# A graph network's scatter of its sorted list, in three parts instead of two

## The chip, the core and the metric

One core of a Trainium2 chip runs the whole program. The metric is the device time of one execution in microseconds (us); lower is better. In a profile, PE is TensorE (PEld its weight loads), DVE VectorE, ACT ScalarE, POOL GpSimd, SP SyncE, and a trailing q marks an engine's sequencer.

## The reference

Four graph layers over 6250 nodes with 128 features and 106250 edges (`src`, `dst`, sorted by `dst`), each added to x after a layer norm and a relu:

```python
h = relu(layernorm(x)); x = x + L0(h)   # hyperbolic linear map, sum over edges, maps back
h = relu(layernorm(x)); x = x + L1(h)   # graph attention (4 heads, softmax per dst), then 25 spiking steps
h = relu(layernorm(x)); x = x + L2(h)   # per edge type: sums at dst of x[src], and at src of x[dst], dense
h = relu(layernorm(x)); x = x + L3(h)   # two weighted graph convolutions with layer norms
```

L1's spikes, for each node and feature, with the attention's output h:

```python
mem = 0.9 * mem + h; spk = mem > 1; mem = mem - spk      # 25 times; result sum(spk) / 25
```

L2 sums in both directions. The edges come sorted by `dst`, so the sum at `src` needs the same list sorted by `src`: the kernel sorts it itself.

## The kernel before

**Data.** Nodes lie in 49 blocks of 128 (NB = 49), in 7 groups of 7 blocks (NG, GB). The padded edges are 832 tiles of 128 (NT), four tiles to a chunk (CT), 208 chunks (NCH), and loops take four chunks a turn (RING), 52 turns (NIT).

**Walks.** Each walk gathers rows from a table in DRAM by 832 indirect DMAs, which GpSimd issues (`walk`, line 598), into a ring of four chunks in GATHERED. VectorE makes one-hot matrices (`onehots`, line 1278), TensorE multiplies them with the rows (`sums`, line 707, eight matmul records a chunk), and VectorE adds the PSUM bank to the block's sum (line 1300, in `aggregate`), then gives the buffer free (line 1322). Walks in order: l0, g1 (the scores' walk), l2, l2b, l3a, l3b. A walk waits until its table is stored.

**The sort.** Beside the l0 walk VectorE works out each edge's place in the list sorted by `src` (PLACE) and the pair to be stored there (REC: key and source). Then `scatter` (line 611) has GpSimd issue one indirect DMA a tile: 128 writes of 8 bytes from REC into `list_dram` at PLACE. Tiles go in batches of 16 (BATCH) on two semaphores in turn (`listed`), and before a batch GpSimd waits for the batch two before it. SyncE reads the list back into REC (line 553) once all are written; it is used from the l2b walk on.

**GpSimd's order around the change.** l0 walk; scatter of tiles 0 to 95 (EARLY = 96) beside the dense work of L1; g1 walk; scatter of tiles 96 to 831; wait for the typed table's stores (`typed_stored`); l2 walk; l2b walk; l3a and l3b.

**The stages beside it.** After the g1 walk (whose rows SyncE stored to `gat_rows` on the way), VectorE and TensorE work out the softmax maxima in unrolled code. The attention's pass ("gb") then goes over all chunks again in a loop: SyncE loads the chunk from `gat_rows` (line 543, 264 KB), ScalarE takes the exponentials (line 1012), VectorE weighs the rows (`weigh`, line 1654) and makes the one-hots, TensorE multiplies, VectorE adds (line 1300). Each addition raises `walks["gb"].added` by one, from 2 to NCH + 2. This pass needs nothing of GpSimd.

After it come the spikes, unrolled: 7 groups by 25 steps. In a step VectorE makes the new membrane and the reset in two halves (lines 1725 and 1729), ScalarE cuts off what is over the threshold (line 1046) and takes its sign (line 1017), and TensorE adds the spikes in PSUM with the identity (two matmuls, line 838). ScalarE's spike n waits with `spk_counted` for TensorE's spike n - 2. VectorE's membrane waits for ScalarE's line 1046 of the step before last. Beside the steps of group g, `typed_beside` does the dense work of L2 for group g - 1 (transposes at line 813, products at 820 and 828, copies at 1037), and SyncE stores each block's typed rows (line 549). The last of these 49 stores frees GpSimd for the l2 walk.

**The dense work of L1**, beside the early scatter: per group TensorE transposes (line 690), ScalarE copies (line 921), TensorE multiplies (line 697), ScalarE copies out (lines 934 and 935).

Of the kernel before, what the change touches and what calls it, by code (L numbers as in the profile page):

```python
# [58 lines left out]
def program(nc, x, src, dst, etype, weight, w0, b0, w1, att_src, att_dst, b1,  # L59
# [14 lines left out]
    NT = RP * RK  # L74
    NCH = NT // CT
# [19 lines left out]
    assert NB <= BUCKETS - 2  # L95
    BATCH = 16
    EARLY = 6 * BATCH
    assert NT % (2 * BATCH) == 0
    NBP = NB + 1
    NP3 = 3  # L100
# [15 lines left out]
    with ctx:  # L116
# [105 lines left out]
        class Walk:  # L222

            def __init__(self, n, gathers=True, adds=True, rounds=0, gathered=None, like=None):
# [4 lines left out]
                if not adds:  # L230
# [8 lines left out]
        walks = {"l0": Walk("l0"), "g1": Walk("g1", adds=False), "ga": Walk("ga", gathers=False, adds=False),  # L239
                 "gb": Walk("gb", gathers=False), "l2": Walk("l2")}  # L240
# [330 lines left out]
        @block.gpsimd  # L571
        def _(pool):
            pool.memset(ONE[:, :], 1.0).then_inc(s_const, 1)
            pool.memset(IDENT[:, :], 0.0).then_inc(s_const, 1)
            pool.memset(LOWER[:, :], 1.0).then_inc(s_const, 1)
            pool.iota(IOTA[:, :], pattern=[[1, NBP * P]], base=0, channel_multiplier=0,
                      allow_small_or_imprecise_dtypes=True).then_inc(s_const, 1)
            pool.iota(PB[:, :], pattern=[[P, NBP]], base=0, channel_multiplier=1,
                      allow_small_or_imprecise_dtypes=True).then_inc(s_const, 1)
            pool.wait_ge(s_const, 3)  # L580
            pool.affine_select(out=IDENT[:, :], in_=IDENT[:, :], compare_op=ALU.not_equal, fill=1.0,
                               base=0, pattern=[[-1, P]], channel_multiplier=1).then_inc(s_const, 1)

            pool.affine_select(out=LOWER[:, :], in_=LOWER[:, :], compare_op=ALU.is_gt, fill=0.0,
                               base=0, pattern=[[-1, P]], channel_multiplier=1).then_inc(s_const, 1)
            pool.iota(KCOL[:, :], pattern=[[1, BUCKETS]], base=0, channel_multiplier=0,
                      allow_small_or_imprecise_dtypes=True).then_inc(s_const, 1)
            pool.iota(CHUNK_AT[:, :], pattern=[[1, 1]], base=0, channel_multiplier=CE,
                      allow_small_or_imprecise_dtypes=True).then_inc(s_const, 1)

            def walk(name, table, width, rows):

                wk = walks[name]
                for c in range(NCH):
                    u = c % RING
                    pool.wait_ge(wk.free, c + 1)
                    for t in range(CT):
                        pool.indirect_dma_start(out=G3[:, u * CT + t, 0:width], out_offset=None, in_=table,  # L598
                                                in_offset=bass.IndirectOffsetOnAxis(
                                                    ap=rows[:, c * CT + t:c * CT + t + 1], axis=0),  # L600
                                                ).then_inc(wk.gathered[u], 16)

            pool.wait_ge(s_stored, 16)
            walk("l0", row_tabs[0], D, SRCI)
            def scatter(tiles):

                for t in tiles:
                    turn, k = divmod(t // BATCH, 2)
                    if t % BATCH == 0 and turn:
                        pool.wait_ge(listed[k], turn * (16 * BATCH))  # L610
                    pool.indirect_dma_start(out=list_dram,  # L611
                                            out_offset=bass.IndirectOffsetOnAxis(ap=PLACE[:, t:t + 1], axis=0),
                                            in_=REC[:, 2 * t:2 * t + 2], in_offset=None).then_inc(listed[k], 16)

            pool.wait_ge(placed, 1)
            scatter(range(EARLY))
            pool.wait_ge(s_stored, 16 * (NG + 1))
            walk("g1", gat_tab, XW, SRCI)
            scatter(range(EARLY, NT))

            for k in range(SLOTS):
                pool.wait_ge(typed_stored[k], 16 * len(range(k, NB, SLOTS)))
            walk("l2", typed_tab, D, KEYI)
            pool.wait_ge(nb_stored, 16 * (NB + 1))
            walk("l2b", typed_b_tab, D, PLACE)
            pool.wait_ge(s_stored, 16 * (2 * NG + 1))
            walk("l3a", row_tabs[1], D, SRCI)
            pool.wait_ge(s_stored, 16 * (3 * NG + 1))
            walk("l3b", row_tabs[2], D, SRCI)
# [1160 lines left out]
```

## Time and profile before

| what | us |
|---|---|
| device time, three runs | 10340.84, 10372.93, 10419.57 |
| median | 10372.93 |
| span of the profiled execution | 10508.5 |

The page gives no other time for the profiled execution than its span; nothing else of note lies around it, so the span is taken as its time. It is 1.3% over the median. "remote" as a releaser means that the profile found no event of this core that ended the wait; "issue" that it found nothing waited for.

### The profile page before, as it was taken

What the parts mean: (1) busy time and instruction counts of PE and PEld (TensorE: products, weight loads), DVE (VectorE), ACT (ScalarE), POOL (GpSimd) and SP (SyncE); (2) the same over time, 40 slices, a digit from 0 to 9 for tenths busy, and PEclk for the clock granted to TensorE, in tenths of its full rate; (3) what the DMA queues carried; (4) which work ended last, traced back from release to release, by engine and by line L of the source; (5) the groups of instructions that cost most, each with busy time, mean ns of one, the idle gap of its engine ahead of it and who ended that gap; (6) DMA issues with size and microseconds to landing.
All of it is one profiled execution on the core that took longest, in us unless ns stands there. A gap on an engine that the chain in (4) does not pass through costs nothing. (4 is left out here: it accounts for less than half of the span.)

```text
span 10508.5 us, 91849 instructions
## 1 busy us (share of the span) xinstructions
PE 3373.1 (32%) x14814; PEld 2819.9 (27%) x14815; DVE 3220.4 (31%) x6992; ACT 1117.8 (11%) x1899; POOL 5762.9 (55%) x5837
## 2 busy tenths in 40 slices
PE   1333431000010103654444443333333333333332
PEld 1333321000000003531233333333333233333332
DVE  5335553000020003579521221121222222422224
ACT  1000002222210000137300000000000000100000
POOL 0666775555567772000366666666655555455554
PEclk6555555555555555756666655555555555555555
DMA  1111112334320001310122221111111111111111
GB/s 39 48 44 42 44 34 74 105 103 106 102 66 11 10 11 49 85 42 28 50 57 56 55 55 42 45 43 45 41 48 40 41 40 41 40 40 40 41 41 40
DMA packets 335299, 521.81 MB, mean 50 GB/s; under 512 B 121171, under 2 KB 187559, under 8 KB 335199
## 3 DMA queue, kind: packets, MB, share of 16 engines
q0 software_dynamic: 186368, 330.08, 12.8%
q1 hardware_dynamic: 148831, 190.78, 5.9%
q14 instruction: 84, 0.69, 0.0%
q8 instruction: 16, 0.26, 0.0%
HBM read 421.31 MB, written 99.13 MB: 50 GB/s over the span
## 5 line engine op out<-in xcount | busy, mean ns | idle before, releaser
L707 PE MATMUL PS<-GATHERED,OH 128*128 128x128 f32 (+1 forms) x10240 | 2417.3, 417 | 4000.8 <-DVE OH L1278 1374.0
L598 POOL DMA_INDIRECT GATHERED<-row_tab,SRCI x2496 | 2465.6, 988 | 1866.8 <-issue 736.5
L707 PEld LDWEIGHTS PS<-GATHERED,OH 128*128 128x128 f32 x10240 | 2144.9, 312 | 4321.0 <-issue 1595.9
L598 POOL DMA_INDIRECT GATHERED<-typed_tab,KEYF x832 | 815.3, 980 | 1501.9 <-DMA typed_tab<-GATHERED 1096.3
L598 POOL DMA_INDIRECT GATHERED<-gat_tab,SRCI x832 | 788.0, 947 | 586.7 <-DVEq L1598 321.9
L598 POOL DMA_INDIRECT GATHERED<-typed_b_tab,PLACE x832 | 811.6, 975 | 430.1 <-issue 241.5
L611 POOL DMA_INDIRECT list_dram<-REC,PLACE x832 | 875.5, 1052 | 275.5 <-issue 275.5
L1284 DVE TENSOR_SCALAR OH<-IOTA,DSTF,WF 128x128 f32 x2048 | 609.4, 355 | 951.0 <-issue 917.8
L707 PE MATMUL PS<-T,OH 128*128 128x132 f32 x2048 | 446.8, 394 | 1065.3 <-issue 501.9
L707 PEld LDWEIGHTS PS<-T,OH 128*128 128x128 f32 x2048 | 400.2, 291 | 1111.9 <-issue 669.8
L1300 DVE TENSOR_TENSOR X<-X,PS 128x128 f32 x512 | 146.9, 287 | 1610.2 <-remote 993.6
L1300 DVE TENSOR_TENSOR ACC<-ACC,PS 128x129 f32 (+1 forms) x512 | 148.1, 289 | 1501.7 <-remote 1046.8
L1300 DVE TENSOR_TENSOR T<-T,PS 128x128 f32 x512 | 146.5, 286 | 1028.4 <-PE PS L707 457.9
L759 PE MATMUL PS<-AMP,EQ 128*128 x832 | 56.4, 177 | 1157.3 <-ACT EQ L978 871.6
L1278 DVE TENSOR_TENSOR OH<-IOTA,DSTF 128x512 f32 (+1 forms) x512 | 354.6, 693 | 146.1 <-issue 137.3
L759 PEld LDWEIGHTS PS<-AMP,EQ 128*128 128x128 bf16 x832 | 38.3, 107 | 1175.6 <-issue 1175.6
L1571 DVE TENSOR_REDUCE EX<-PS 128x48 f32 x208 | 43.2, 208 | 1006.0 <-issue 492.5
L900 ACT ACTIVATE H<-T,DINV 128x128 f32<-128x128 f32 x98 | 29.9, 394 | 2707.9 <-DVEq L56 2707.9
L974 ACT ACTIVATE SCR<-ROWI,SM 128x512 bf16<-128x512 int16 x208 | 150.0, 721 | 860.3 <-issue 850.3
L1278 DVE TENSOR_TENSOR OH<-IOTA,REC 128x512 f32 (+1 forms) x256 | 177.6, 694 | 197.2 <-issue 195.5
L838 PE MATMUL PS<-ACC,WSB 128*128 128x448 bf16 x350 | 145.2, 515 | 283.4 <-ACT ACC L1017 283.4
L1278 DVE TENSOR_TENSOR OH<-IOTA,SM 128x512 f32 (+1 forms) x256 | 177.2, 692 | 173.1 <-issue 171.1
(263 smaller groups left out, 3070.2 us busy)
## 6 DMA issues: line engine op xcount, KB each, us to landing
gat_rows<-GATHERED SPq DMA_DIRECT2D x208, 264.0 KB
GATHERED<-gat_rows SPq DMA_DIRECT2D x208, 264.0 KB
GATHERED<-row_tab,SRCI POOLq DMA_INDIRECT x2496
ROWI<-dst_rows SPq DMA_DIRECT2D x208, 128.0 KB
list_dram<-REC,PLACE POOLq DMA_INDIRECT x832
GATHERED<-gat_tab,SRCI POOLq DMA_INDIRECT x832
GATHERED<-typed_tab,KEYF POOLq DMA_INDIRECT x832
GATHERED<-typed_b_tab,PLACE POOLq DMA_INDIRECT x832
```

The costliest lines, as they stand in the source:

```text
L598: pool.indirect_dma_start(out=G3[:, u * CT + t, 0:width], out_offset=None, in_=table, in_offset=bass.IndirectOffsetOnAxis(ap=rows[:, c * C ...
L611: pool.indirect_dma_start(out=list_dram, out_offset=bass.IndirectOffsetOnAxis(ap=PLACE[:, t:t + 1], axis=0), in_=REC[:, 2 * t:2 * t + 2], ...
L707: last = mm(bank(p)[:, 0:r.shape[1]], onehot(p, t), r, start=(t == 0), stop=(t == CT - 1))
L759: last = mm(bank(k)[:, t * AW:(t + 1) * AW], onehots_[:, t * P:(t + 1) * P], AMP[:, bass.ds(b * AW, AW)], start=True, stop=True)
L838: last = mm(SPIKES[:, k, :], IDB, SPK[t % 2][:, k * (GB * D // 2):(k + 1) * (GB * D // 2)], start=(t == 0), stop=(t == LIF_T - 1))
L900: last = nc.scalar.activation(H3[:, b, :], T3[:, b, :], ACT.Copy, scale=DINV[:, b:b + 1])
L974: nc.scalar.activation(SCRB[:, CE:2 * CE], ROWI[:, u * CE:(u + 1) * CE], ACT.Abs, bias=NODE[:, bass.ds(first, 1)], scale=float(FAR)).then_ ...
L1278: return v.tensor_tensor(onehot(p, 0, CT).rearrange("p (t w) -> p t w", t=CT), IOTA[:, bass.ds(b * P, P)].rearrange("p (o w) -> p o w", o= ...
L1284: last = v.tensor_scalar(onehot(p, t), IOTA[:, bass.ds(b * P, P)], DSTF[:, bass.ds(c * CT + t, 1)], weights[:, bass.ds(c * CT + t, 1)], AL ...
L1300: return v.tensor_tensor(dest, dest, bank(p)[:, 0:F], ALU.add)
L1571: return v.tensor_reduce(o, bank(k)[:, 0:n * NP3].rearrange("p (t i k) -> p t k i", t=CT, i=NP3), axis=AX.X, op=ALU.add)
```

## The change

The tiles 96 to 431 stay behind the scores' walk. GpSimd then waits until the attention's pass has made its last addition, and issues tiles 432 to 831 after that. 96 tiles come ahead of the scores' walk, 336 behind it and 400 behind the pass.

```diff
     EARLY = 6 * BATCH
+    MIDDLE = EARLY + 21 * BATCH
@@
             scatter(range(EARLY))
             pool.wait_ge(s_stored, 16 * (NG + 1))
             walk("g1", gat_tab, XW, SRCI)
-            scatter(range(EARLY, NT))
+            scatter(range(EARLY, MIDDLE))
+            pool.wait_ge(walks["gb"].added, NCH + 2)
+            scatter(range(MIDDLE, NT))
```

## Rows read from the trace of the kernel before

**Rows 1.** The page: busy us (share of span) of each engine

```profile
PE 3373.1 (32%) x14814; PEld 2819.9 (27%) x14815; DVE 3220.4 (31%) x6992; ACT 1117.8 (11%) x1899; POOL 5762.9 (55%) x5837
```

**Rows 2.** Busy time in stretches: window, length, engines, clock, DMA share, GB/s

```profile
3117.50:4034.80 917.30, 88.99 (x352) 79.13 (x352) 67.72 (x122) 18.88 (x43) 690.53 (x673) 0.51 0.06 12
...
4063.00:4613.00 550.00, 355.31 (x1688) 319.19 (x1688) 316.27 (x592) 90.10 (x210) 0.00 (x0) 0.68 0.30 82
...
4632.00:5131.00 499.00, 221.27 (x595) 77.97 (x595) 450.70 (x789) 364.30 (x422) 0.00 (x0) 0.62 0.07 27
```

**Rows 3.** Line 611's tiles (POOL), whole and in stretches; then line 1654 in stretches

```profile
L611 POOL DMA_INDIRECT list_dram<-REC,PLACE x832: 966/972/6518, 1509.3 to 4033.8; - x167
...
1509.30:1651.30 142.00, 112.11 (x96) 0.54 0.05 8
3028.00:4034.80 1006.80, 761.42 (x734) 0.51 0.06 12
...
3200.00:4000.00 800.00, 20.14 (x29) 0.51 0.06 11
4100.00:4600.00 500.00, 107.72 (x156) 0.68 0.31 84
```

**Rows 4.** Waits of line 1300 in 3200:4000, then in 4100:4600: total, times, longest

```profile
DVE ACC L1300 <- remote: 737.0, 36, 21.3
...
DVE ACC L1300 <- PE PS L707: 151.0, 109, 2.4
```

**Rows 5.** Timeline of the attention's pass: start, us, engine, operation [idle before <-releaser]

```profile
3597.76 2.10 PE L707 MATMUL PS<-T,OH 128*128 128x132 f32 x8 [19.72 <-issue]
...
3617.75 0.29 DVE L1300 TENSOR_TENSOR ACC<-ACC,PS 128x132 f32 x1 [20.30 <-remote]
...
4060.85 0.29 DVE L1300 TENSOR_TENSOR ACC<-ACC,PS 128x132 f32 x1 [15.41 <-remote]
...
4063.59 2.10 PE L707 MATMUL PS<-T,OH 128*128 128x132 f32 x8 [15.73 <-DVE ACC L1300]
```

**Rows 6.** Timeline beside the early scatter, the dense work of L1

```profile
1637.35 0.92 ACT L921 ACTIVATE ROWI<-PS 128x896 f32<-128x896 f32 x1 [9.18 <-remote]
...
1641.56 0.93 PE L690 MATMUL PS<-IDENT,H 128*128 128x128 f32 x7
...
1653.57 0.92 ACT L921 ACTIVATE ROWI<-PS 128x896 f32<-128x896 f32 x1 [13.33 <-remote]
...
1657.87 1.24 PE L690 MATMUL PS<-IDENT,H 128*128 128x128 f32 x7
...
1659.15 0.92 ACT L921 ACTIVATE ROWI<-PS 128x896 f32<-128x896 f32 x1 [2.70 <-PE PS L690]
```

**Rows 7.** Line 598 (POOL): ns min/median/max, first and last start

```profile
L598 POOL DMA_INDIRECT GATHERED<-typed_tab,KEYF x832: 942/947/1455, 5131.0 to 6351.0; - x167
L598 POOL DMA_INDIRECT GATHERED<-typed_b_tab,PLACE x832: 941/947/1444, 6360.7 to 7592.7; - x167
```

**Rows 8.** Timeline of the first group's spikes, about one step

```profile
4655.71 0.93 ACT L1017 ACTIVATE ACC<-ACC 128x896 bf16<-128x896 f32 x1
4655.72 1.15 DVE L1725 SCALAR_TENSOR_TENSOR ACC<-ACC,T 128x448 f32<-128x448 f32 x2
...
4656.70 0.93 PE L838 MATMUL PS<-ACC,WSB 128*128 128x448 bf16 x2 [1.22 <-ACT ACC L1017]
4656.79 1.15 DVE L1729 SCALAR_TENSOR_TENSOR ACC<-ACC 128x448 f32<-128x448 f32 x2
```

**Rows 9.** Timeline of the softmax maxima: tiles of the scatter beside VectorE's scans

```profile
3065.25 2.29 DVE L1610 TENSOR_TENSOR_SCAN H<-ACC,H 104x1024 f32<-104x1024 f32 x1
3065.80 2.51 POOL L611 DMA_INDIRECT list_dram<-REC,PLACE  x1 [0.30 <-issue]
...
3067.95 2.29 DVE L1608 TENSOR_TENSOR_SCAN H<-ACC,PS 104x1024 f32<-104x1024 f32 x1
3068.62 0.97 POOL L611 DMA_INDIRECT list_dram<-REC,PLACE  x1 [0.30 <-issue]
```

## The prediction

> **What bounds the kernel now.** I read the page first: no engine is busy over 55% of the span [rows 1], so shares decide nothing and the stages must be read one by one. Around the change the order is this: early scatter (1509 to 1651, [rows 3]), the scores' walk to 3028, the softmax maxima to 3117, the attention's pass to 4613, the spikes from 4632 [rows 2], and the next walk at 5131 [rows 7]. All 736 later tiles of the scatter sit behind the scores' walk: 734 of them in 1006.8 us, or 1.371 us a tile [rows 3].
>
> The attention's pass has two paces. VectorE's weighing (line 1654) runs once a chunk: 29 times in 800 us while GpSimd scatters, 156 times in 500 us afterwards [rows 3]. That is 27.6 us a chunk against 3.2 us. The last tile is issued at 4033.8, and the last slow addition comes 26 us after its end, at 4060.85 [rows 3, 5], so the scatter sets the pace. The DMA engines are not full (share 0.06, against 0.30 at the fast pace), and VectorE is busy 68 us in 917 [rows 2]. 
>
> The same is seen beside the early scatter, in unrolled code without loads of the pass [rows 6]: the transposes of line 690 end at 1642.49 and ScalarE, which waits for them, starts at 1653.57, 11.1 us later. Once no tile is issued, the next pair is 1659.11 and 1659.15, no delay at all. The same wait in the group before is 9.18 us, and 13.33 in this one: the delay grows from group to group.
>
> **The change, part by part.** It changes no instruction of the work, only the place of 400 of 832 tiles on GpSimd's queue, and it adds one wait, on the semaphore of the attention's additions.
>
> 1. *Out of the attention's pass.* 400 tiles by 1.371 us are 548 us. In that time the pass did 548 / 27.6 = 20 chunks, which take 20 x 3.2 = 64 us at the fast pace. Gain: 548 - 64 = 484 us. This is the firmest term; its bounds are 450 (if some delay were left at the end of the shorter scatter, another 26 us of draining as in [rows 5], which exists before as well) and 490.
>
> 2. *The added wait.* Behind it on GpSimd stand the 400 tiles, then the wait for the typed table and the next walk. Nobody needs the tiles before SyncE reads the list for the second walk, some 1200 us later [rows 7], so the wait itself costs nothing. But the next walk can't start before the 400th tile is issued. From the last addition (about 4613) to the walk (5131) are 517 us; the tiles take 548 us at 1.371 us, and 592 at the 1.48 us of the early scatter (96 tiles in 142 us, [rows 3], where VectorE also has long operations). So 31 to 75 us are lost even if nothing else is slowed. SyncE's read of the list stands behind the typed stores and moves with them; its stores of the typed table leave the DMA engines at a share of 0.07 [rows 2].
>
> 3. *What the tiles do to the spikes.* This is the open term. A step of the spikes is 2.14 us when nothing is beside it (lines 1725 and 1729 begin 1.07 us apart, [rows 8]): four VectorE operations, two of ScalarE, two matmuls. Over the whole stage it is 2.70 us: from 4632 to 5104, 472 us, for 175 steps. The rest of the stage is 19 us ahead (4613 to 4632) and 27 us behind (5104 to 5131). ScalarE's spike n waits for TensorE's count of spike n-2, so an answer that comes d late makes a step about (d + 2.1) / 2 us, where 2.1 are the spike and its two matmuls (0.93 + 0.93, and the hand-over, [rows 8]). The lower bound for d is 0, as at 1659 [rows 6]; the upper one is the whole pace of the attention's pass. The nearest row is that of unrolled code with TensorE, ScalarE and VectorE all at work, the 11.1 us of [rows 6]; I take it. A step is then (11.1 + 2.1) / 2 = 6.6 us.
>
>    The sum: the delay needs time to build. 19 us pass before the first matmul of the stage, and I give it 20 us more (7 steps), since it grew over about three groups in [rows 6]. The other 510 us of scatter hold 510 / 6.6 = 77 steps. After the last tile the delay drains for 26 us, as from 4034.8 to 4060.85 [rows 5], with 4 steps. The remaining 175 - 88 = 87 steps take 235 us, the tail 27. Stage: 548 + 26 + 235 + 27 = 836 us in place of 517, a loss of 319 us. It contains the 31 us of point 2.
>
> 4. *Net.* 319 - 484 = -165 us. The profiled execution has a span of 10508.5 us, 136 us (1.3%) over the median of the runs, 10372.9; I take the difference as it is, so 10372.9 - 165 = 10208 us, 1.6% less.
>
> **Two rules weighed against the trace.** Rows 4 to 6 show TensorE's answers coming late beside the scatter. The Trainium skill (SBUF — State Buffer, Who interferes with whom) says that PE and ACT never wait on anyone and that a DMA doesn't contend with a compute engine; by that rule point 3 would be nil, and the result that of rival B. The trace disagrees on the answers, though it agrees that the matmuls themselves are not stretched: 2.10 us for eight in both [rows 5].
>
> **Rivals.**
>
> *A. Every answer is as late as in the attention's pass (slower side).* There two groups of matmuls were in flight and the pace was still 22 to 28 us, so the delay was not shared between them. A step of the spikes then costs 27.6 us, not 6.6, and VectorE holds GpSimd up to 1.48 us a tile. Then 592 us of scatter hold 7 + (554 / 27.6 =) 20 steps, 1 more in the draining; 147 are left, 397 us. Stage 592 + 26 + 397 + 27 = 1042, a loss of 525, net +41 us: 10414 us. It decides from a step of about 16 us upwards at that pace of tiles (132 steps left give a stage of 1001 us, a loss of 484); at 22 us and 1.371 us a tile the net is still -11. For it: the cycle VectorE, ScalarE, TensorE exists in both stages. Against: in [rows 6] the delay was smaller.
>
> *B. The spikes are hardly slowed.* The delay appears when GpSimd runs at full pace. Where VectorE has an operation with both inputs in SBUF, a tile waits for its end: 2.51 us in place of 0.97 beside line 1610, and 0.97 beside line 1608, whose one input is PSUM [rows 9]. In the spikes all four VectorE operations are of the first kind, so the tiles may come slowly enough for TensorE's answers to stay prompt, at 1.48 us a tile (point 2). Then only the 75 us of point 2 are lost: 484 - 75 = 409 us gained, 9964 us.
>
> *C. VectorE starves GpSimd.* The same rows [rows 9], but worse: VectorE's spike operations follow each other without a gap (two take 1.15 us, and the next two begin after 1.07, [rows 8]). If a tile gets through once in a step of 2.70 us, 175 are done in the spikes, and 225 are left at the full pace of 1.27 us (0.97 and 0.30 of idling, [rows 9]), or 286 us, ahead of the walk. Net 286 - 484 = -198, 10175 us. With none at all in the spikes, 508 us are left: +24. The skill's page on SBUF (same section) has this as a rule: an exclusive lock against a GpSimd instruction that reads SBUF when VectorE has two SBUF inputs. By that rule C is the case and not the forecast; the rows show the lock for long operations only.
>
> *D. The change doesn't do what it says:* the pass stays slow through a cause that only coincides with the scatter. The pace turns too near to 4034.8 for that; time as before.
>
> **How the numbers follow.** Chances: forecast 0.35, A 0.25, B 0.20, C 0.15, D 0.05. The range 9960 to 10420 takes in A and B, the two bounds of point 3, and leaves out mishaps beyond them and a scatter that is free altogether. A measurement of this kernel tells some 1% (104 us) from no change. Faster by over 1%: 0.26 of the forecast's 0.35 (d up to about 16 us), B whole, 0.13 of C, 0.01 besides, 0.60. Within 1%: 0.09 of the forecast, 0.17 of A, the rest of C and D, 0.31. Slower by over 1%: 0.08 of A, where a second answer of TensorE in the same step (the typed work) comes late too and outlasts the scatter, and 0.01 besides, 0.09.
>
> **What would show each step.** Right: 336 tiles end near 3486; the attention's pass ends near 4130 with 150 chunks or more at 3.2 us; no wait of line 1300 for an unnamed releaser after 3520; then 400 tiles. In the spikes, ScalarE's line 1017 waits 9 to 13 us for an unnamed releaser, beginning some 40 us into the stage and ending 26 us after the last tile; the next walk starts some 165 us earlier than 5131. For A, waits of 17 us and more once a step. For B, line 838's answers prompt and GpSimd's last tile ahead of the walk by a few us. For C, tiles of over 2 us, and a row of tiles behind the last spike. The prediction is wrong in its largest term if the pass isn't at 3.2 us a chunk after 3520.

## The result, and the profile after

The changed kernel takes 9983.99 us (median of four runs, 9938.06 to 10042.51), the kernel before 10373.61 in its four: a ratio of 0.963, 95% interval 0.9595 to 0.9664, or 390 us less. The forecast was 10208 us, 165 us less. The profiled execution's span is 9962.4 us.

Windows of the changed kernel (as [rows 2]: the attention's pass beside the tiles and without them, the spikes, and what follows the last typed store; columns are PE, PEld, DVE, ACT, POOL busy, clock, DMA share, GB/s):

```profile
3084.00:3436.00 352.00, 37.51 (x152) 33.45 (x152) 29.03 (x52) 8.16 (x18) 266.89 (x270) 0.52 0.07 16
3463.00:4063.00 600.00, 386.09 (x1825) 348.36 (x1826) 341.85 (x640) 98.92 (x230) 0.00 (x0) 0.67 0.31 83
4101.00:4570.00 469.00, 205.59 (x554) 70.40 (x554) 435.14 (x770) 354.54 (x407) 375.39 (x302) 0.62 0.08 25
4613.00:4694.00 81.00, 0.00 (x0) 0.00 (x0) 0.00 (x0) 0.11 (x1) 60.94 (x63) 0.50 0.03 4
```

The last line is new: 63 tiles in 81 us with no other engine at work. Next line 1657 alone, the weighing (once a chunk), in the first two of these windows, as [rows 3]:

```profile
3084.00:3436.00 352.00, 11.07 (x16) 0.52 0.07 16
3463.00:4063.00 600.00, 127.42 (x184) 0.67 0.31 83
```

Three lines of the code by their instructions (number, ns min/median/max, first and last start): the tiles (now line 612), the first halves of the spikes (1728) and the typed stores (550):

```profile
L612 POOL DMA_INDIRECT list_dram<-REC,PLACE x832: 967/972/7145, 1521.1 to 4693.3; - x167
...
L1728 DVE SCALAR_TENSOR_TENSOR ACC<-ACC,T x350: 617/625/629, 4101.3 to 4569.6; 128x448 f32<-128x448 f32 x175
...
L550 SPq DMA_DIRECT2D typed_tab<-GATHERED x49: 319/319/332, 4202.0 to 4612.9; - x49
```

The pass does 16 chunks in 352 us beside tiles that follow each other every 1.30 us (22 us a chunk), and 184 in 600 us behind them (3.26 us). The 175 steps of the spikes, with 302 tiles beside them, run from 4101.3 to 4569.6, which is 468 us; before, without a tile, they ran from 4632.2 to 5100.2, which is 468 us as well:

```profile
L1725 DVE SCALAR_TENSOR_TENSOR ACC<-ACC,T x350: 611/617/627, 4632.2 to 5100.2; 128x448 f32<-128x448 f32 x175
```

Waits of the addition (line 1303, as [rows 4]) in 3200 to 3430, then in 3550 to 4050:

```profile
DVE ACC L1303 <- remote: 205.0, 10, 21.3
...
DVE ACC L1303 <- PE PS L710: 152.9, 101, 2.4
```

And the timeline from the pass's end, GpSimd's tiles among the other engines' work (as [rows 8, 9]):

```profile
4083.28 0.97 POOL L612 DMA_INDIRECT list_dram<-REC,PLACE  x1 [647.00 <-DVE ACC L1303]
...
4085.58 6.69 DVE L1092 TENSOR_TENSOR T<-ACC,SM 128x6272 f32<-128x6272 f32 x1
...
4086.14 6.99 POOL L612 DMA_INDIRECT list_dram<-REC,PLACE  x1 [0.30 <-issue]
...
4107.93 1.30 POOL L612 DMA_INDIRECT list_dram<-REC,PLACE  x1 [0.30 <-issue]
4109.54 1.30 POOL L612 DMA_INDIRECT list_dram<-REC,PLACE  x1 [0.30 <-issue]
...
4184.20 0.93 PE L841 MATMUL PS<-ACC,WSB 128*128 128x448 bf16 x2 [1.05 <-ACT ACC L1020]
...
4595.26 0.60 ACT L1040 ACTIVATE GATHERED<-PS 128x512 f32<-128x512 f32 x1 [8.93 <-remote]
...
4693.25 0.97 POOL L612 DMA_INDIRECT list_dram<-REC,PLACE  x1 [0.30 <-issue]
4694.53 0.99 POOL L599 DMA_INDIRECT GATHERED<-typed_tab,KEYF  x1 [0.31 <-issue]
```

Beside a spike's operations, whose two inputs lie in SBUF, a tile takes 1.30 us in place of 0.97 and the next starts 1.61 us after it. No engine waits there for an unnamed releaser. When VectorE has done its spikes the tiles return to 0.97 us, and TensorE's answers are late again, in unrolled code: ScalarE's copy at 4595.26 waits 8.93 us, and two later ones 0.85 and 2.98 us, for an unnamed releaser, where the same first copy waited 5.15 us for TensorE before:

```profile
5121.98 0.60 ACT L1037 ACTIVATE GATHERED<-PS 128x512 f32<-128x512 f32 x1 [5.15 <-PE PS L828]
```

The l2 walk starts at 4694.53, 81.6 us behind the last typed store, where it was 2.4 us before (5128.6 to 5131.0).

**The account.** From the first weighing to the last addition the pass took 1496.1 us (3117.4 to 4613.5) and takes 997.6 (3085.1 to 4082.7): 498.5 gained. From there to the l2 walk it was 517.5 and is 611.8: 94.3 lost. Net 404 us, near the 390 of the medians. The spans differ by 546, because the two executions also differ where nothing was changed (the walks l3a and l3b 1346 and 1339 us before, 1275 and 1282 after).

### The profile page after: what moved, and what is told of

It is laid out like the page before. It is cut to its first block and busy times, and to the rows that moved or that the text cites. A ratio compares the mean times of both kernels' runs of the same rounds, so it can differ in the third digit from the quotient of the medians.

```text
span 9962.4 us, 91850 instructions
## 1 busy us (share of the span) xinstructions
PE 3387.4 (34%) x14814; PEld 2831.8 (28%) x14815; DVE 3213.4 (32%) x6992; ACT 1119.2 (11%) x1899; POOL 5827.7 (58%) x5837
## 3 DMA queue, kind: packets, MB, share of 16 engines
q0 software_dynamic: 186368, 330.08, 13.8%
## 5 line engine op out<-in xcount | busy, mean ns | idle before, releaser
L612 POOL DMA_INDIRECT list_dram<-REC,PLACE x832 | 942.2, 1132 | 907.6 <-DVE ACC L1303 647.0
L903 ACT ACTIVATE H<-T,DINV 128x128 f32<-128x128 f32 x98 | 29.9, 396 | 2584.0 <-DVEq L56 2584.0
```

Source lines behind the costliest of these rows:

```text
L612: pool.indirect_dma_start(out=list_dram, out_offset=bass.IndirectOffsetOnAxis(ap=PLACE[:, t:t + 1], axis=0), in_=REC[:, 2 * t:2 * t + 2], ...
L903: last = nc.scalar.activation(H3[:, b, :], T3[:, b, :], ACT.Copy, scale=DINV[:, b:b + 1])
```

## The experiments

The experiments ran on six chips, here A to F, each beside the kernel before. Where several executions were timed in turn with it, the ratio stands with its 95% interval; the other times are of a single execution. Medians in us:

| chip | kernel before | kernels on it, with ratio and interval |
|---|---|---|
| A | 10371.97 | e1_nops 9953.88; e2_batch2 9912.78; e3_two_a_chunk 9663.33, 0.9315 (0.9266 to 0.9363); e4_memset 9666.93 |
| B | 8319.13 | e5_paced 8315.53, 0.9998 (0.9988 to 1.0007); e6_doses 8313.36; e7_early_paced 8341.54, 1.0026 (1.0017 to 1.0036); e8_few_rows 8760.12 |
| C | 10337.94 | e9 (the change) 9944.33, 0.9621 (0.9575 to 0.9666); e10 (as e5) 9542.18, 0.9224 (0.9181 to 0.9267) |
| D | 10522.91 | e11_probe 10115.48; e12 (the change) 10130.00, 0.9640 (0.9609 to 0.9670); e13 (as e7) 9681.92 |
| E | 10356.56 | e14_paced_best 9511.68, 0.9174 (0.9128 to 0.9220); e15_walk_doses 9608.87; e16 (the change) 9955.79, 0.9616 (0.9571 to 0.9661) |
| F | 8316.65 | e17 (the kernel before) 8314.57; e18 (the change) 8411.28, 1.0111 (1.0094 to 1.0128) |

**Chip A: distance, backlog or the loop?** The question is why the same tiles delay TensorE's answers beside the pass and not beside the spikes. Theory P says: the distance of the tiles, from start to start, is what counts (1.30 us in the pass, 1.61 in the spikes). Q says it is the loop and its loads, R the number of tiles outstanding. The diffs here and below are cut to the lines that matter, and most leave out the lines of the change that they replace.

```diff
e1, e4: behind each tile in scatter(range(176, 256)), (256, 336), (336, 416)
+    for _ in range(nops): pool.nop(nofuse=True)        # e1: 16, 8, 4
+    pool.memset(FILL[:, 0:fill], 0.0)                  # e4: 1024, 640, 320 bf16
e2
-    BATCH = 16
+    BATCH = 2
e3
+    scatter(range(EARLY, 160))
+    for c in range(NCH):
+        pool.wait_ge(walks["gb"].added, c + 2)
+        scatter(range(160 + 2 * c, 162 + 2 * c))
+    scatter(range(160 + 2 * NCH, NT))
```

> The tiles 176 to 415 get idle instructions on GpSimd's queue behind each one (16, then 8, then 4, for 80 tiles each), tiles 416 to 495 none; tile 496 waits for the pass's last addition. Theory P (pace): TensorE's answers come late only where tiles follow each other at the full pace of about 1.3 us; with a tile every 1.6 us or more, as in the spikes, the attention's pass runs near 3.2 us a chunk beside them, and turns slow (20 us and more a chunk) only where the idle instructions are few or none. Theory Q (the loop and its loads): any tile beside the pass makes it slow, at whatever pace, so it stays at 20 us and more a chunk until the last tile before the wait.

> The changed kernel with batches of 2 tiles in place of 16, so that at most 4 tiles are outstanding in place of 32. Theory R (backlog): the delay is that of a queue of outstanding tiles; with 4 of them the attention's pass falls well below 20 us a chunk although tiles still come at 1.3 to 1.4 us each. Theory P: if the pace of tiles stays at 1.4 us or less, the pass stays slow as in the changed kernel (27 us a chunk); it gets fast only if the waits stretch a tile to 1.6 us or more.

> Tiles 96 to 159 behind the scores' walk at full pace, then two tiles for each addition of the attention's pass (416 tiles in 208 chunks), the last 256 behind it. Theory P: the pass holds about 3.2 us a chunk with a tile each 1.6 us and takes about 670 us for all its chunks, as against 998 us in the changed kernel; the last 256 tiles at 1.61 us (412 us) end before the last typed store, so the 82 us tail goes too: 400 us less than the changed kernel, about 9590 us. Theory Q: the pass is slow whenever a tile is beside it, and the wait only ties them: two tiles a chunk of 20 us or more, 4000 us and more in all, a far slower kernel. Theory R: two to four outstanding tiles, so fast as with P.

> As the one with idle instructions, but a GpSimd memset of 1024, 640 and 320 bf16 columns behind each tile instead. Theory P: what matters is the distance of tiles, so the same course against the distance as there. If instead GpSimd's being busy or its port is what delays TensorE's answers, the pass stays slow at every distance here and not there.

The idle instructions changed no distance: the 80 tiles with 16 of them behind each start within 102.9 us, where the kernel before's own took 102.7, and the pass makes 12 chunks in 350 us. The trace of e1 has 91850 instructions, as many as the changed kernel's, and none of the 2240 idle ones among them, so it doesn't show whether they ran at all. e1 tests nothing. Batches of 2 kept tiles at 1.30 us (193 in 250 us) and the pass slow, 9 chunks in the same 250 us, with at most 4 tiles outstanding in place of 32: theory R falls. The memsets did change the distance. Of e4, the weighing in 3236 to 3336 (1024 columns, at its end 640), 3486 to 3586 (320) and 3636 to 3686 (none again), then the tiles in the same three:

```profile
3236.00:3336.00 100.00, 20.79 (x30) 0.67 0.32 84
3486.00:3586.00 100.00, 21.47 (x31) 0.70 0.33 84
3636.00:3686.00 50.00, 1.39 (x2) 0.50 0.06 12
...
3236.00:3336.00 100.00, 49.36 (x48) 0.67 0.32 84
3486.00:3586.00 100.00, 66.74 (x62) 0.70 0.33 84
3636.00:3686.00 50.00, 38.24 (x39) 0.50 0.06 12
```

At a tile every 2.08 and every 1.61 us the pass runs at 3.2 to 3.3 us a chunk; at 1.28 it falls to 25 (2 in 50 us). GpSimd is no less busy with a memset than without, so it isn't its being busy; and the loop and its loads are the same: theory Q falls, P stands. e3, with two tiles for each addition, took 785 us for the pass (3104.5 to 3889.6) where 670 were expected. Its tiles come in bursts, 1.28 us apart inside a burst, and its addition waits 64 us, in 32 times, for an unnamed releaser; that the bursts cause it is argued, not shown. It takes 709 us less than the kernel before, where the change takes some 390.

**Chip B: the paced kernel, finer doses, fewer rows.**

```diff
e5
+    scatter(range(EARLY, 160))
+    scatter(range(160, 560), 320)                      # memset of 320 columns behind each
+    pool.wait_ge(walks["gb"].added, NCH + 2)
+    scatter(range(560, NT))
e6: 256, 192, 128, 64, 0 columns, 80 tiles each, in place of 320
e7: e5, and
-    scatter(range(EARLY))
+    scatter(range(EARLY), 320)
e8, beside the pass, all whole tiles from 160 on behind it
+    few(range(160, 288), 64)                           # PLACE[0:64, t], REC[0:64, ...]
+    few(range(288, 448), 16)
```

> Tiles 96 to 159 at full pace, 160 to 559 beside the attention's pass with a GpSimd memset of 320 bf16 columns (0.38 us) behind each, the last 272 behind the pass's last addition. Theory P (pace of tiles): the pass runs at 3.2 to 3.3 us a chunk from its first chunks on, 680 to 700 us in all, against 785 us with two tiles a chunk and 994 us in the changed kernel; no tail of tiles behind the last typed store (272 tiles by 1.61 us are 438 us). About 9560 us. If the two-a-chunk kernel's gain came from its waits on the pass and not from the distance of tiles: slow again, at or above the changed kernel's 9984 us.

> The same places, with memsets of 256, 192, 128, 64 and no columns for 80 tiles each. Theory P with a sharp bound: the pass is at 3.2 us a chunk down to some distance between 1.6 and 1.3 us a tile (the run with 1024 to 320 columns was in between at 1.43), and at 20 us or more a chunk beyond it, within a few tiles. A gradual law instead: the time of a chunk rises from dose to dose, 4, 6, 10 us.

> The kernel with paced tiles, and the 96 early tiles, beside the dense work of L1, paced by the same memset. Theory P: the answers of TensorE to ScalarE (transposes of the dense work), 9 to 13 us late in the kernel before, are prompt in this unrolled stage without loads too; the 96 tiles take 96 by 1.6 = 154 us in place of 142, the dense work ends before them, and the scores' walk starts some 10 to 25 us earlier after the l0 walk's end than the 166 us of before: 10 to 25 us less than the paced kernel. Theory Q' (lateness in this stage has another cause): the answers stay late, and the stage takes 165 us or more.

> Beside the attention's pass, additional stores of the first 64 rows of 128 tiles, then (from its 79th addition) of the first 16 rows of 160 tiles, back to back; all whole tiles from 160 on come behind the pass (so more tiles in all, and the time is longer by some 280 us of additional tail; output unchanged). What is the load that makes TensorE's answers late? Theory I (instructions): one DMA issued after the other with no gap is enough, so the pass is slow beside both. Theory W (rows, the descriptors written per us): if the stores of 64 and 16 rows are hardly shorter than 0.97 us, the rate of rows is a half and an eighth, and the pass is fast at least beside those of 16 rows.

All four forecasts missed, because their premise was gone: on this chip the kernel before takes 8319 us and nothing is late. The pass runs at 3.2 to 3.3 us a chunk beside everything: 93 chunks in 300 us beside 208 tiles in e6, 197 in 650 us beside the small stores of e8. e5 gains nothing, and e7, whose early memsets only lengthen the scatter there, loses 22 us. The 8760 us of e8 hold its extra stores and its later tiles and say nothing by themselves.

**Chip C: the change and the paced kernel again.**

> The changed kernel itself. The last four kernels ran on a chip on which the kernel before takes 8319 us and not 10372, and on which TensorE's answers are never late, tiles or no tiles. Theory K (the lateness belongs to some chips): on such a chip the attention's pass runs at 3.2 us a chunk beside the tiles, so moving 400 of them out of it gains nothing, and the change only adds the tail of tiles behind the last typed store: 70 to 95 us slower than before, about 8400 us. On a chip where the kernel before takes about 10370 us, the pass is slow until some 20 us behind the last of its tiles, and the change gains 350 to 430 us again. Rival: the lateness comes and goes on every chip, so the same kernel shows both within one call.

> The kernel with paced tiles again. On a chip where the kernel before takes about 10370 us, theory P (pace of tiles) expects the pass at 3.2 to 3.3 us a chunk from its first chunks on, and no tail: about 9560 us, 100 less than with two tiles a chunk. On a chip where the kernel before takes 8319 us: 8315 us again, no gain, and 90 us less than the changed kernel, for want of its tail.

Here the answers are late again, and both forecasts hold: the change gains 394 us (0.9621), the paced kernel takes 9542 us where 9560 were expected. Its pass lasts 680 us (3090.9 to 3770.5), with 375 tiles in 600 us beside 181 chunks.

**Chip D: the doses, the rows, and unrolled code.** e11 puts 64 tiles each with memsets of 256, 192, 128 and 64 columns beside the pass, then 32 plain ones, 96 stores of 64 rows and 96 of 16; e13 is e7 again.

> Beside the attention's pass, in this order: 48 tiles at full pace (most ahead of the pass), 64 tiles each with a memset of 256, 192, 128 and 64 bf16 columns behind every tile, a pause until the pass has added chunk 140, 32 tiles at full pace, a pause, 96 additional stores of 64 rows, a pause, 96 of 16 rows; then the remaining 400 whole tiles behind the pass. Extra work of 192 stores and more tiles late, so the time itself tells nothing. On a chip where the kernel before takes about 10350 us: theory P with a sharp bound expects 3.2 us a chunk down to some distance between 1.6 and 1.3 us a tile and 20 us and more a chunk below it; a gradual law expects a rise from dose to dose. Theory I (an instruction with no gap is enough): slow beside the stores of 64 and of 16 rows, if these follow at 1.3 us. Theory W (rows written per us): fast beside those of 16 rows at least. On a chip where the kernel before takes 8319 us all of them leave the pass at 3.2 us.

> The changed kernel on whatever chip this call gets. Theory K (the lateness belongs to some chips): if the kernel before takes 8319 us here, the change is 70 to 95 us slower, about 8400 us, with a pass at 3.2 us a chunk throughout and a tail of 60 to 75 tiles behind the last typed store; if it takes about 10350 us, some 390 us faster, as in both calls so far.

> The kernel with paced tiles in which the 96 early tiles, beside the dense work of L1, have the memset of 320 columns behind them too. On a chip where the kernel before takes about 10350 us, theory P: TensorE's answers to ScalarE are prompt there too, the scatter's 96 tiles take 154 us, and the scores' walk starts 155 to 160 us behind the end of the l0 walk in place of 167. Theory Q' (the lateness of this stage has another cause): 9 to 13 us late as before, and the walk starts 167 us or more behind it.

Weighings of e11 in the stretches of 256, 192, 128 and 64 columns, of the stores of 64 rows and of 16; then the tiles in the four doses; then the small stores in their two stretches:

```profile
3075.00:3177.00 102.00, 18.75 (x27) 0.60 0.31 81
3177.00:3275.00 98.00, 18.06 (x26) 0.61 0.29 73
3275.00:3368.00 93.00, 12.58 (x19) 0.57 0.22 53
3368.00:3456.00 88.00, 4.85 (x7) 0.50 0.11 25
3750.00:3865.00 115.00, 4.16 (x6) 0.51 0.07 15
3942.00:4052.00 110.00, 4.89 (x7) 0.52 0.08 17
...
3075.00:3177.00 102.00, 70.60 (x64) 0.60 0.31 81
3177.00:3275.00 98.00, 68.00 (x64) 0.61 0.29 73
3275.00:3368.00 93.00, 66.67 (x65) 0.57 0.22 53
3368.00:3456.00 88.00, 63.36 (x63) 0.50 0.11 25
...
3750.00:3865.00 115.00, 86.04 (x96) 0.51 0.07 15
3942.00:4052.00 110.00, 81.19 (x95) 0.52 0.08 17
```

By distance: 1.59 us a tile gives 3.1 us a chunk (27 from the pass's first weighing, at 3094.7), 1.53 gives 3.8, 1.43 gives 4.9, 1.40 gives 12.6, and the changed kernel's 1.30 gave 22. The loss begins near 1.5 us, and most of it comes below 1.45. These are means of one stretch each, in one order, and at 1.40 the delay was still building: from 3367 on the weighings are 3.1, 6.7, 13.8, 17.2, 11.3, 9.4 and 23.5 us apart. (The 32 plain tiles, in 40 us with 5 weighings, are too short a stretch for more.) So the distance from which the delay comes is seen only roughly, and whether 1.40 would end at the full 22 us is open. The small stores follow every 1.20 and 1.16 us and leave 19 and 16 us a chunk. These means hold prompt chunks at their start: once the delay is there, the weighings are 19 to 23 us apart, and once in each stretch 41 to 44, beside 64 rows, beside 16, and beside whole tiles in the changed kernel as well. An eighth of the rows does the same. Theory W (rows written) falls, I (instructions) stands: what counts is how often GpSimd issues a DMA, not how much it writes.

In the dense work of L1, ScalarE's line 924 waits 31.1 us in three times for an unnamed releaser in e12, as in [rows 6]. With the 96 early tiles paced (e13, line 932) that line has no such wait left in the whole program (its instructions, and what ended the idle time before them):

```profile
L932 ACT ACTIVATE ROWI<-PS x21: 917/918/918, 1584.1 to 8270.5; 128x896 f32<-128x896 f32 x21
...
  PE PS L701: 54.2, 19
  issue: 3.6, 2
```

So the same holds in unrolled code, and Q' (another cause in this stage) falls; e10, whose early tiles are not paced, still has 29.9 us of such waits at this line. The walk came no sooner, though: the 96 tiles took 177 us, not 154, and the walk starts 177 us behind the l0 walk (168 in e12). In e12 GpSimd waits 24.6 us behind its last early tile for the store of the scores' table; in e13 it waits for nothing there, as the slower tiles themselves end last.

**Chip E: fewer early tiles, and pauses in the walks.**

```diff
e14
-    EARLY = 6 * BATCH
+    EARLY = 4 * BATCH
@@
+    scatter(range(EARLY), 320)
@@
+    scatter(range(EARLY, 128))
+    scatter(range(128, 544), 320)
+    pool.wait_ge(walks["gb"].added, NCH + 2)
+    scatter(range(544, NT))
e15: e14, and a memset behind each gather of a walk: g1 64, l2 128, l2b 192, l3a 64, l3b 256
```

> The paced kernel with 64 early tiles, paced, in place of 96 at full pace; 64 tiles behind the scores' walk at full pace, 416 paced beside the pass, 288 behind it. Theory P: with the early tiles paced TensorE's answers in the dense work of L1 are prompt (as seen with 96), and 64 tiles at 1.83 us end after 117 us, so the scores' walk starts 120 to 135 us behind the end of the l0 walk in place of 167; pass and spikes as in the paced kernel, 288 tiles by 1.61 us being 464 us of some 500. On a chip where the kernel before takes about 10350 us: ratio to it 0.918, 0.004 less than the paced kernel's 0.922. On one where it takes 8319 us: within 1% of before.

> The same, and the gathers of the walks paced too, each walk by another memset behind every gather: g1 64 columns, l2 128, l2b 192, l3a 64, l3b 256 (l0 none). Theory P carried to the walks: there GpSimd also issues at full pace, and waits for buffers that VectorE gives free late, because TensorE's answers are late; a gather takes 1.47 to 1.57 us in place of 1.25. With a short pause the answers come in time, and a gather costs 1.31 us (64 columns), 1.37 (128), 1.42 (192) or 1.48 (256): walks of 1090, 1140, 1180 and 1230 us against 1220 to 1305. If at 64 columns the answers are still late, g1 and l3a stay at 1.5 us. Rival: a walk is bound by GpSimd alone, and every pause lengthens it by its own 0.03 to 0.23 us a tile.

> The changed kernel once more, for the chip of this call. Theory K (the lateness belongs to some chips): if the kernel before takes 8319 us here, the change is 70 to 95 us slower, about 8400 us; if it takes 10300 to 10550 us, about 390 us faster.

e14 is as forecast: the scores' walk starts 126 us behind the l0 walk's end, the pass takes 672 us, the l2 walk follows the last typed store by 2.5 us, and the ratio is 0.917 where 0.918 was expected. It has the lowest ratio on a chip with late answers, though its interval meets that of e10; it was not tried on one without. In e15 neither theory has all its numbers. The walks g1 (64 columns), l2 (128), l2b (192), l3a (64) and l3b (256) take 1384, 1255, 1219, 1307 and 1223 us against 1312, 1227, 1263, 1310 and 1250 in e14. With 256 columns the walk comes out as theory P has it (1230): GpSimd waits 15 us for buffers in l3b, 188 in e14, and VectorE's addition 223 us for an unnamed releaser, 404 in e14. With 192 it is 44 us shorter than in e14, which the rival (every pause lengthens a walk) excludes. With 64 and 128 P's numbers fail, as its own text allows for 64. So the answers get less late, but a pause long enough for that costs GpSimd nearly what it saves, and the walks stay near 1.5 us a gather; one execution shows this, and the kernel as a whole took 9608.87 us, more than e14.

**Chip F: the sign.**

> The kernel before, profiled on the chip of this call. If the chip runs it in 8319 us: the attention's pass at 3.2 us a chunk beside tiles at 1.3 to 1.4 us, no wait of line 1300 for an unnamed releaser. If in 10300 to 10550 us: the profile of before once more, 27 us a chunk beside the tiles.

> The changed kernel, for the chip of this call. Theory K (the lateness belongs to some chips): where the kernel before takes 8319 us, 70 to 95 us slower, about 8400 us, for the tail of tiles behind the last typed store; where it takes 10300 to 10550 us, about 390 us faster.

A second chip without late answers, and the change is 1.1% slower there: 8411.28 us against 8316.65, 95 us, as theory K (the lateness belongs to some chips) had it. The kernel before on it (e17): weighings, then tiles in the pass,

```profile
2664.00:3344.00 680.00, 143.26 (x206) 0.63 0.33 82
...
2664.00:3344.00 680.00, 524.81 (x493) 0.63 0.33 82
```

and the waits of line 1300 there, where [rows 4] had 737.0 us for an unnamed releaser:

```profile
DVE ACC L1300 <- PE PS L707: 214.5, 145, 2.4
DVE ACC L1300 <- issue: 0.9, 5, 0.2
```

206 chunks at 3.3 us beside 493 tiles at 1.38. There is nothing to gain by moving tiles. The change on the same chip (e18) has its last typed store at 3858.0; the tiles behind it:

```profile
3858.00:3954.00 96.00, 72.00 (x75) 0.52 0.03 6
```

These 75 tiles in 96 us are its loss: the l2 walk starts 96.2 us behind the last typed store, and 2.5 us behind it in e17.

## Why the prediction was right or wrong

- **What bounds the kernel** was right where the kernel before takes 10340 us and more: late answers of TensorE, only while GpSimd issues back to back [rows 4 to 6]. It holds on A, C, D and E, and not on B and F, which no row of one profile can show.
- **Point 1** (484 us, bounds 450 and 490): 498.5 measured, 8 us over the upper bound. The mechanism is right.
- **Point 2** (31 to 75 us): right in kind, too small. It took the tiles' distance as 1.371 to 1.48 us; it was 610 us for 400 tiles, 1.53 each (1.55 in the spikes, 302 in 469 us). The loss is 94 us. Of it 15 us arise in the last group's typed work, where the late answers are: from the last spike to the last typed store 28.4 us before, 43.3 after, and all of the difference lies between its copies at lines 1034 and 1040 (4585.4 to 4612.3, and 5115.9 to 5127.9 before).
- **Point 3 is the step that failed.** It took the delay d = 11.1 us from [rows 6] as that of the spikes, a step at 6.6 us, and a loss of 319 us for the stage. Measured are d = 0 and steps as before. The row was chosen by the form of its stage (unrolled, three engines at work). What decides is the distance of the tiles: 1.28 us around [rows 6], 1.61 in the spikes. Nor was 11.1 us a steady value: the four groups' answers in that stage come 0, 3.1, 6.1 and 11.1 us late, still growing when the tiles end. On chip D the pass ran at 3.1 us a chunk at 1.59 us a tile, and at 12.6 at 1.40. That the spikes themselves would be slowed at 1.30 us a tile was not tried; the typed work right behind them, at 1.28 us a tile, is slowed. The right row was there, [rows 9], where an operation with two SBUF inputs holds a tile; rival B read it so and gave 9964 us, 20 below the measured 9984, at a chance of 0.20.
- **Point 4**: 319 - 484 = -165 becomes 94 - 498 = -404 by measured terms; the medians give -390.
- **Rival A** falls with point 3. **Rival C**: the hold exists (0.97 to 1.30 us a tile, and 6.99 beside the 6.69 us operation at 4085.58), but GpSimd gets through 1.7 times in a step of 2.70, not once. The exclusive lock that the Trainium skill states (SBUF — State Buffer, Who interferes with whom) for two SBUF inputs is thus seen here beside short operations too, and it was what saved the change: it spaces the tiles. **Rival D** is refuted on A, C, D and E.
- By the Trainium skill (SBUF — State Buffer, Who interferes with whom) PE and ACT never wait on anyone; by that point 3 was nil, and nil it was. But on the chips with late answers the engines behind TensorE do wait, some 20 us at a time beside back-to-back tiles (21.3 us at most in line 1303), which that rule doesn't cover.
- The range (9960 to 10420) held the time, though the forecast's reason did not: it reached down to rival B's 9964. What no chance of the forecast held is the chip's part in the sign: 0.962 to 0.964 on four chips, 1.011 on F.

## What to carry to other kernels

When an engine's stream disturbs another stage, price it by the row with the same distance between its instructions, not by the row whose code looks alike. Before moving such a stream away, try to space it: a small memset of 0.38 us behind each tile beside the pass left pass and spikes at full pace (ratio 0.922, and 0.9998 where there was nothing to win), while moving left a tail that costs 1.1% on a chip without the effect. And time a change that lives from waits for an unnamed releaser on more than one chip.

## What was not expected of the hardware

- **Chips differ by 20% on this kernel.** 8317 and 8319 us on two, 10338 to 10523 on four. The surplus goes with late answers: in e17 line 1300 has no wait for an unnamed releaser in the whole program, where before's trace has 2389 us of them (1046.8, 993.6 and 348.9 for its three targets). The walks g1, l2, l2b take 1037, 1063 and 1076 us in e5 and 1350, 1220 and 1232 in the trace of before. In all, the six walks and the attention's pass take 2147 us less in e17 than in before's trace, of 2196 us between the two spans. What makes it so stays open. Each chip was seen for one short time only, in which all executions agreed, so a condition that would pass with more time is not told apart from the chip.
- **The delay is that of the DMA's issuing, not of its rows or of GpSimd's work**: a store of 128, 64 or 16 rows takes 0.97, 0.90 or 0.84 us, each with 0.30 us behind it, and the three delay alike; 4 outstanding tiles do the same as 32; and with a memset between the tiles GpSimd is busier and the answers are prompt.
- **The delay takes time to build.** It is 0, 3.1, 6.1 and 11.1 us in the last four groups beside the early scatter before it ends, and in the pass it reaches some 20 us and stays there.
- **VectorE can hold a tile over many operations.** In e17, in the spikes, one took 30.75 us, from 3390.63 to 3421.38, while VectorE's operations followed each other without a gap; VectorE fell idle 2.71 us before its next one at 3423.25. The tile lay there on no path.

```profile
3387.95 1.31 POOL L611 DMA_INDIRECT list_dram<-REC,PLACE  x1 [0.30 <-issue]
3390.63 30.75 POOL L611 DMA_INDIRECT list_dram<-REC,PLACE  x1 [1.37 <-issue]
...
3423.25 1.09 DVE L1735 TENSOR_SCALAR T<-PS 128x896 f32<-128x896 f32 x1 [2.71 <-PE PS L838]
```
